# A four-layer graph network on one core: longer lags between producers and consumers, byte flags kept in SBUF, and the last layer's product moved ahead of its scan

## The chip, the cores and the metric

The kernel runs on one core of a Trainium2 chip. The metric is the device time of one execution in microseconds (us). A run of the kernel before takes 7871.08 us, the median of three (7854.48 to 7896.73).

## The reference, cut to what matters

The graph has 100,000 nodes and 50,000 edges sorted by receiver (`dst`), and 128 channels per node, all f32. Four graph layers follow each other, each with a residual and a layer norm over the channels:

```python
edge_index = jnp.stack([src, dst])
x = _layernorm(x + _L0_gnn_ref(x, edge_index, ...))        # attention over 4 heads
x = _layernorm(x + _L1_gnn_ref(x, Wq, Wk, Wv, Wo, edge_index))   # N = 625 nodes in its own formula, all edges
x = _layernorm(x + _L2_gnn_ref(x, edge_index, W0, b0, W1, b1))   # two degree-normalised layers with relu
x = _layernorm(x + _L3_gnn_ref(x, edge_attr_3, edge_weight, src, dst, 100000, ...))   # messages, segment sum, W_out0/W_out1
```

In all of them the messages of the edges with the same receiver are summed (`segment_sum`). In the last one a message has 256 channels (64 scalars and 64 vectors of 3), and the sum is multiplied by the output weights, which leaves 128 channels. A node that receives no edge takes part only through its own row.

## The kernel before

The 50,000 edges are padded to 50,176 = 98 items of 512 edges (4 chunks of 128 edges, one edge per partition). The core works through twelve stages, each with its own buffers and semaphores and a barrier behind it. The change touches the last four, and two small stages ahead of them. In the trace the tiles have these prefixes:

- `ats` is `second_layer`: load the messages `xs`, weight them (GpSimd, `weight`), turn them so that channels lie on partitions (TensorE, `turn`), running sum along the edges (VectorE, `scan`), product with `wvo` (TensorE, `multiply`), add and layer norm (VectorE `add` and `scale`, ScalarE `norm_root` and `apply`, GpSimd `widen`), store.
- `gs0` is `gcn_first`: gather rows by index (GpSimd, four indirect DMAs an item), turn and accumulate with the own rows, scan, product with `w0`, `take`, `activate`, store.
- `gs1` is `gcn_second`: the same with `w1`; a product with only four weight rows (`root` and `blocks`) adds the bias; relu, residual and norm follow.
- `mss` is `final_edges`: gather, scale and turn the sender's row (`scale_x`, `turn_x`, `copy_x`), `project`, build the message of 2 x 128 channels (`messages`), turn both halves (`turn_sums`), two scans, eight products with `wout` (`reduce`), `combine`, norm, and a scatter to the output (GpSimd, four indirect DMAs an item).
- `l0` (`first_layer`), `asc` (`attention_scores`) and `rad` (`radial_basis`) come before these.

The scan multiplies the running sum by a flag that is 0 where a new receiver begins and adds the next message. The flags stand in one line in DRAM, `T["cont"]`, as f32; each of the four stages loads 512 of them per item, copied to all 128 partitions (256 KB), in the same `load` as its other inputs.

Each engine runs a program of its own, written with `pipeline(engine, (part, lag), ...)`: in slot q it does each part, in the order listed, for item q minus its lag. The engines meet only through semaphores (`wait_ge`, and `wait_item(..., 4)` for a buffer that item minus 4 must have left; there are `BUFS = 4` buffers, and two PSUM buffers `tp` and `hp`). An engine's queue is in order, so a waiting part holds up all that stand behind it. In `ats` the lags before are:

```python
            pipeline(sp, (load, 0), (store, 5))
            pipeline(pool, (widen, 3), (weight, 0))
            pipeline(pe, (multiply, 1), (turn, 0))
            pipeline(act, (apply, 4), (lambda t, u: norm_root(norm, act, t, u), 3))
            pipeline(dve, (scan, 0), (add, 1), (scale, 2))
```

`load` there waits for `weighted`, `scanned` and `summed` of the item four back, and then issues all three loads. `apply` writes two tables from `y`: the next layer's input (`t12`, rows of 132 floats, 528 bytes) and the residual (`x2`, rows of 512 bytes), each by four activations. GpSimd's `scatter` in `mss` follows its gathers by `SCATTER_LAG = 4` items.

Of the kernel before, what the change touches and what calls it, by code (L numbers as in the profile page):

```python
# [15 lines left out]
ALU = mybir.AluOpType  # L16
# [25 lines left out]
SCATTER_LAG = 4  # L42
# [143 lines left out]
def edge_line(table, t, u):  # L186

    return table[0:1, bass.ds(t * (4 * BUFS * P) + u * 4 * P, 4 * P)].broadcast_to([P, 4 * P])
# [11 lines left out]
def prepare(nc, A, T, K):  # L200

    with ExitStack() as ctx:
# [15 lines left out]
        same = sb("same", [P, 4, P])  # L218
        final = sb("final", [P, 4, P])
# [42 lines left out]
        def _(sp):  # L262
# [23 lines left out]
            for tile, a, off in [(cur, 1, 0), (nxt, 1, 1), (srow, 0, 0)]:  # L286
# [4 lines left out]
                         same[0:rows].rearrange("p b i -> p (b i)")).then_inc(cont_stored, 16)  # L291
# [3 lines left out]
        def _(act):  # L295
# [10 lines left out]
            act.dma_start(T["cont"][0:1, 0:1], zeros[0:1, 0:1]).then_inc(cont_stored, 16)  # L306
# [33 lines left out]
        def _(dve):  # L340
# [13 lines left out]
            dve.memset(K["row0"][0:1, :], 1.0)  # L354
            dve.memset(K["one"][:], 1.0)
# [21 lines left out]
            dve.tensor_tensor(same[0:rows], cur[0:rows], nxt[0:rows], ALU.is_equal).then_inc(same_ready, 1)  # L377
# [767 lines left out]
def gat_sums(nc, A, T, K):  # L1145
    with ExitStack() as ctx:
# [38 lines left out]
        def _(dve):  # L1185
# [28 lines left out]
            link(dve.tensor_scalar(K["degepsB"][:], K["totB"][:, HEADS, :], 1.0, EPS * D, ALU.add, ALU.mult))  # L1214
# [368 lines left out]
def second_layer(nc, A, T, K):  # L1583
    with ExitStack() as ctx:
# [4 lines left out]
        cont = [sb(f"cont{u}", [P, 4 * P]) for u in range(BUFS)]  # L1589
# [3 lines left out]
        o2 = [sb(f"o2{u}", [P, 4, D]) for u in range(BUFS)]  # L1593
        rsz, nbz = [sb(f"rsz{u}", [P, 4]) for u in range(BUFS)], [sb(f"nbz{u}", [P, 4]) for u in range(BUFS)]
        rsx, nbx = [sb(f"rsx{u}", [P, 4]) for u in range(BUFS)], [sb(f"nbx{u}", [P, 4]) for u in range(BUFS)]
        tp = [ps(f"tp{v}", [P, 4, P]) for v in range(2)]
        hp = [ps(f"hp{v}", [P, 4, D]) for v in range(2)]
        xs_loaded, own_loaded, cont_loaded, weighted = sems("xs_loaded"), sems("own_loaded"), sems("cont_loaded"), sems("weighted")
        turned, scanned, multiplied, summed = sems("turned"), sems("scanned"), sems("multiplied"), sems("summed")
        stored, x_stored, o_set, zero_set = sems("stored"), sems("x_stored"), sem("o_set"), sem("zero_set")  # L1600
# [5 lines left out]
        def _(sp):  # L1606
            def load(t, u):
# [3 lines left out]
                sp.dma_start(xs[u][:], edge_rows(T["xsrc"], t, u)).then_inc(xs_loaded[u], 16)  # L1611
                sp.dma_start(cont[u][:], edge_line(T["cont"], t, u)).then_inc(cont_loaded[u], 16)
                sp.dma_start(own[u][:], edge_rows(T["t12"][0:EP], t, u)[:, :, 0:D]).then_inc(own_loaded[u], 16)

            def store(t, u):
                sp.wait_ge(applied[u], t + 1)
                sp.dma_start(edge_rows(T["t12"][T12_Z:T12_Z + EP], t, u), o[u][:]).then_inc(stored[u], 16)
                sp.dma_start(edge_rows(T["x2"], t, u), o2[u][:]).then_inc(x_stored[u], 16)
            pipeline(sp, (load, 0), (store, 5))
            for u in range(BUFS):  # L1620
                sp.wait_ge(stored[u], 16 * PER_BUF[u])
                sp.wait_ge(x_stored[u], 16 * PER_BUF[u])

        @block.gpsimd
        def _(pool):
# [5 lines left out]
            def widen(t, u):  # L1631
# [3 lines left out]
                pool.tensor_tensor(nbz[u][:], norm["nb"][u][:], four(K["dlastB"], t, u), ALU.mult)  # L1635
                pool.tensor_tensor(rsx[u][:], norm["rs"][u][:], four(K["dsqrtB"], t, u), ALU.mult)
                pool.tensor_tensor(nbx[u][:], norm["nb"][u][:], four(K["dsqrtB"], t, u), ALU.mult).then_inc(widened[u], 1)
            pipeline(pool, (widen, 3), (weight, 0))

        @block.tensor  # L1640
        def _(pe):
# [574 lines left out]
```

## Time and profile before

| | |
|---|---|
| runs | 7854.48, 7871.08, 7896.73 us |
| profiled execution | 7874.37 us, of which the span of the core is 7872.4 us |
| TensorE matmul | 4003.5 us busy (51%) |
| VectorE | 3570.1 us (45%) |
| GpSimd | 3751.2 us (48%) |
| ScalarE | 2687.6 us (34%) |
| `ats`, 4686 to 5374 us | 688 us |
| `gs0`, 5374 to 5973 us | 599 us |
| `gs1`, 5973 to 6590 us | 617 us |
| `mss`, 6590 to 7872 us | 1282 us |

No engine is busy for much over half of the span, so the shares of the whole say little: each stage has its own limit. Dividing a stage by its 98 items gives its pitch, and an engine whose work per item is close to that pitch is what limits it. The clock is TensorE's granted clock as a share of 2.4 GHz; 0.5 is 1.2 GHz.

### The profile page before, as it was taken

How to read it: one execution, taken by the hardware profiler on the slowest of the kernel's cores; microseconds unless marked ns; L12 is line 12 of the kernel's file. 1: busy time of each engine (PE TensorE's matmuls, PEld its weight loads, DVE VectorE, ACT ScalarE, POOL GpSimd, SP SyncE). 2: the span in 40 equal slices, each digit the busy share in tenths (PEclk: the TensorE clock that was granted, in tenths of full speed). 3: DMA queues.
4: the chain of work that ended last, by engine and by line, in shares of the span. 5: the costliest groups of instructions: out<-in, count | busy, mean ns of one | idle time of the engine just before them, and what ended most of it. 6: DMA issues, size and time to landing. Idle time of an engine off the chain costs nothing. (4 is left out here: it accounts for less than half of the span.)

```text
span 7872.4 us, 85274 instructions
## 1 busy us (share of the span) xinstructions
PE 4003.5 (51%) x18822; PEld 3174.7 (40%) x18822; DVE 3570.1 (45%) x12700; ACT 2687.6 (34%) x6766; POOL 3751.2 (48%) x4124
## 2 busy tenths in 40 slices
PE   2444444112961118825468764444556885555555
PEld 1443344101641015514356543333554554555554
DVE  4484444001671005548711135553334665656665
ACT  0014455001861018815433324442222332222222
POOL 3655655775006750003255532225665664666665
PEclk9655555555985559957789975556666666777676
DMA  1236666111851016624455547776777996333333
GB/s 51 64 89 184 185 191 188 36 19 48 262 174 34 21 39 216 216 64 132 110 132 151 158 129 193 190 192 155 178 180 183 220 218 150 98 101 98 101 98 79
DMA packets 1395766, 1048.50 MB, mean 133 GB/s; under 512 B 171017, under 2 KB 1232586, under 8 KB 1395521
## 3 DMA queue, kind: packets, MB, share of 16 engines
q1 hardware_dynamic: 1279294, 866.89, 39.6%
q0 software_dynamic: 112896, 179.36, 10.1%
q10 hardware_dynamic: 3458, 1.02, 0.1%
q14 instruction: 86, 0.70, 0.0%
q8 instruction: 32, 0.52, 0.0%
HBM read 603.60 MB, written 448.78 MB: 134 GB/s over the span
## 5 line engine op out<-in xcount | busy, mean ns | idle before, releaser
L985 POOL DMA_INDIRECT t_alpha<-gsm_raw,gsm_edge_idx x392 | 401.8, 1025 | 591.7 <-DVE gsm_raw L1107 467.2
L1128 PE MATMUL gsm_zr<-kept_ident,gsm_zT 128*128 128x128 f32 x784 | 141.0, 307 | 936.8 <-ACT gsm_zT L1030 749.4
L1952 POOL DMA_INDIRECT out_dram<-mss_o,kept_scat_idx x392 | 390.8, 997 | 364.6 <-ACT mss_o L1297 274.0
L511 POOL DMA_INDIRECT sort_xd<-in_x_dram,kept_dst_idx x392 | 378.6, 966 | 382.9 <-DMA t_xdst<-sort_xd 226.6
L1417 POOL DMA_INDIRECT asc_xs<-t_t,kept_idx_a x392 | 370.8, 946 | 354.2 <-issue 120.3
L1336 POOL TENSOR_TENSOR l_xb<-l_x,kept_bias 128x512 f32<-128x512 f32 x98 | 133.5, 1363 | 842.0 <-DMA l_x<-t_xdst 841.3
L741 PE MATMUL sort_sps<-kept_wa,sort_xdT 128*128 128x4 f32 x784 | 221.6, 353 | 607.0 <-ACT sort_xsT L765 572.8
L1128 PEld LDWEIGHTS gsm_zr<-kept_ident,gsm_zT 128*128 128x128 f32 x784 | 89.8, 150 | 986.9 <-ACT gsm_zT L1030 797.3
L1822 POOL DMA_INDIRECT gs_xs<-t_z,kept_idx_a x392 | 370.7, 946 | 237.0 <-issue 94.0
L1724 POOL DMA_INDIRECT gs_xs<-t_t,kept_idx_b x392 | 370.7, 946 | 214.6 <-issue 105.8
L978 POOL DMA_INDIRECT gsm_raw<-t_al,gsm_from_idx x392 | 395.6, 1009 | 161.5 <-issue 129.1
L1960 POOL DMA_INDIRECT mss_xs<-t_x,kept_idx_a x392 | 396.5, 1011 | 150.7 <-issue 119.2
L741 PEld LDWEIGHTS sort_sps<-kept_wa,sort_xdT 128*128 128x128 f32 x784 | 209.5, 327 | 641.0 <-ACT sort_xsT L765 400.3
L1070 DVE SCALAR_TENSOR_TENSOR gsm_y<-gsm_hp,gsm_x 128x512 f32<-128x512 f32 x196 | 135.5, 692 | 697.4 <-remote 569.3
L513 POOL DMA_INDIRECT sort_xs<-in_x_dram,kept_src_idx x392 | 379.4, 968 | 120.3 <-issue 119.9
L1297 ACT ACTIVATE mss_o<-mss_y,mss_nb,mss_rs 128x128 f32<-128x128 f32 x392 | 161.4, 482 | 756.7 <-DVE mss_nb L1289 451.1
L1030 ACT ACTIVATE gsm_zT<-gsm_zp,kept_b0col 128x512 f32<-128x512 f32 x196 | 134.7, 687 | 754.7 <-remote 477.2
L1511 DVE CUSTOM_DVE_ANT_0 asc_prod<-asc_qp,asc_xs 128x128 f32<-128x128 f32 x392 | 90.6, 287 | 557.3 <-remote 269.7
L1973 PE MATMUL mss_xtp<-kept_ident,mss_xk 128*128 128x128 f32 x392 | 106.1, 423 | 447.9 <-ACT mss_xk L2006 423.0
L1297 ACT ACTIVATE gsm_o<-gsm_y,gsm_nb,gsm_rs 128x128 f32<-128x128 f32 x784 | 323.2, 488 | 15.9 <-issue 15.6
L193 PE MATMUL gs_tp<-kept_ident,gs_xs 128*128 128x128 f32 x784 | 303.9, 394 | 46.3 <-issue 29.4
L1996 PE MATMUL mss_op<-kept_wout,mss_sc 128*128 128x128 f32 x1568 | 311.8, 383 | 4.0 <-DVE mss_sc L2045 4.0
(527 smaller groups left out, 12860.5 us busy)
## 6 DMA issues: line engine op xcount, KB each, us to landing
t_t<-sort_o SPq DMA_DIRECT2D x66, 792.0 KB
t_x<-gsm_o SPq DMA_DIRECT2D x196, 264.0 KB
sort_x<-in_x_dram SPq DMA_DIRECT2D x66, 768.0 KB
gsm_x<-t_t SPq DMA_DIRECT2D x196, 256.0 KB
t_z<-gsm_z SPq DMA_DIRECT2D x196, 256.0 KB
out_dram<-gsm_o SPq DMA_DIRECT2D x196, 256.0 KB
gs_cont<-t_cont SPq DMA_DIRECT2D x196, 256.0 KB
t_t<-l_o SPq DMA_DIRECT2D x98, 264.0 KB
```

The costliest lines, as they stand in the source:

```text
L511: pool.indirect_dma_start(xd[u][:, j, :], None, A["x"], bass.IndirectOffsetOnAxis(K["dst_idx"][:, c:c + 1], 0)).then_inc(gathered[u], 16)
L513: pool.indirect_dma_start(xs[u][:, j, :], None, A["x"], bass.IndirectOffsetOnAxis(K["src_idx"][:, c:c + 1], 0)).then_inc(gathered[u], 16)
L741: pe.matmul(sps[:, j, 0:HEADS], xdT[u % 2][:, j, :], K["wa"][:, HEADS:8], start=True, stop=False)
L978: pool.indirect_dma_start(raw[:, c, 0:HEADS], None, T["al"], bass.IndirectOffsetOnAxis(from_idx[:, c:c + 1], 0)).then_inc(gathered[u], 16)
L985: pool.indirect_dma_start(T["alpha"], bass.IndirectOffsetOnAxis(edge_idx[:, c:c + 1], 0), raw[:, c, :], None).then_inc(scattered[u], 16)
L1297: ac = act.activation(norm["o"][u][:, g, :], norm["y"][u][:, g, :], ACT.Identity, bias=norm["nb"][u][:, g:g + 1], scale=norm["rs"][u][:, g ...
L1417: pool.indirect_dma_start(xs[u][:, j, :], None, T["t12"][0:EP + N], bass.IndirectOffsetOnAxis(K["idx_a"][:, c:c + 1], 0)).then_inc(gathere ...
L1724: pool.indirect_dma_start(xs[u][:, j, :], None, T["t12"], bass.IndirectOffsetOnAxis(K["idx_b"][:, c:c + 1], 0)).then_inc(gathered[u], 16)
L1822: pool.indirect_dma_start(xs[u][:, j, :], None, T["z1"], bass.IndirectOffsetOnAxis(K["idx_a"][:, c:c + 1], 0)).then_inc(gathered[u], 16)
L1952: pool.indirect_dma_start(T["out"], bass.IndirectOffsetOnAxis(K["scat_idx"][:, c:c + 1], 0), o[u][:, j, :], None, bounds_check=N - 1, oob_ ...
L1960: pool.indirect_dma_start(xs[u][:, j, :], None, T["x3"], bass.IndirectOffsetOnAxis(K["idx_a"][:, c:c + 1], 0)).then_inc(gathered[u], 16)
L1996: mm = pe.matmul(op[u % 2][:, j, :], sc[u][:, a, j * P:(j + 1) * P], K["wout"][:, a, :], start=(a == 0), stop=(a == parts - 1))
```

## The change

The lags between the parts grow in all four stages and the parts that shared one `load` are split, each with its own wait. The flags become bytes, are loaded once (in `rad`) to a tile of 50,176 bytes on every partition, and the scans read them there; `m0g` and `emb` are freed after `asc` to make room. `ats` no longer writes `x2`; `gs1` reads its residual from `t12` instead, which holds the same rows scaled by `dlastB`, and makes up for the factor with `dinv2B`, the degree term of the norm, and a new ScalarE part, `lift`. In `mss` the product with `wout` is made on the turned message, ahead of the scan: ScalarE copies the turned halves to SBUF (`copy_msg`), TensorE multiplies (`reduce`, two products with 512 moving columns), VectorE scans one row of 128 channels instead of two, and TensorE turns the result back (`turn_back`).

```diff
-SCATTER_LAG = 4
+SCATTER_LAG = 15
...
+def goes_on(K, t, u):
+    return K["cont"][:, bass.ds(t * (4 * BUFS * P) + u * 4 * P, 4 * P)]
...
# prepare
-            dve.tensor_tensor(same[0:rows], cur[0:rows], nxt[0:rows], ALU.is_equal).then_inc(same_ready, 1)
+            link(dve.tensor_tensor(same[0:rows], cur[0:rows], nxt[0:rows], ALU.is_equal))
+            dve.tensor_copy(same8[0:rows], same[0:rows]).then_inc(same_ready, 1)
...
# gat_sums
-            link(dve.tensor_scalar(K["degepsB"][:], K["totB"][:, HEADS, :], 1.0, EPS * D, ALU.add, ALU.mult))
+            link(dve.tensor_tensor(K["dinv2B"][:], K["dinvB"][:], K["dinvB"][:], ALU.mult))
+            link(dve.tensor_scalar(K["degepsB"][:], K["dinv2B"][:], EPS * D, None, ALU.mult))
...
# radial_basis, on SyncE, behind the loads of r and ahead of those of m0g
+            sp.dma_start(K["cont"][:], T["cont"][0:1, 0:EP].broadcast_to([P, EP])).then_inc(cont_loaded, 16)
...
# second_layer
-                wait_item(sp, weighted, t, u, 4)
-                wait_item(sp, scanned, t, u, 4)
-                wait_item(sp, summed, t, u, 4)
-                sp.dma_start(cont[u][:], edge_line(T["cont"], t, u)).then_inc(cont_loaded[u], 16)
-                sp.dma_start(edge_rows(T["x2"], t, u), o2[u][:]).then_inc(x_stored[u], 16)
-            pipeline(sp, (load, 0), (store, 5))
+            pipeline(sp, (load_xs, 0), (load_own, 3), (store, 10))
-                pool.tensor_tensor(rsx[u][:], norm["rs"][u][:], four(K["dsqrtB"], t, u), ALU.mult)
-                pool.tensor_tensor(nbx[u][:], norm["nb"][u][:], four(K["dsqrtB"], t, u), ALU.mult).then_inc(widened[u], 1)
-            pipeline(pool, (widen, 3), (weight, 0))
+            pipeline(pool, (weight, 0), (widen, 6))
-            pipeline(pe, (multiply, 1), (turn, 0))
+            pipeline(pe, (multiply, 3), (turn, 1))
-                    ac = act.activation(o2[u][:, j, :], y[u][:, j, :], ACT.Identity, bias=nbx[u][:, j:j + 1], scale=rsx[u][:, j:j + 1])
-            pipeline(act, (apply, 4), (lambda t, u: norm_root(norm, act, t, u), 3))
+            pipeline(act, (lambda t, u: norm_root(norm, act, t, u), 5), (apply, 7))
-            pipeline(dve, (scan, 0), (add, 1), (scale, 2))
+            pipeline(dve, (scan, 2), (add, 4), (scale, 5))
...
# gcn_first: no cont load; the parts otherwise as before
-            pipeline(sp, (load, 0), (store, 3))
+            pipeline(sp, (load, 0), (store, 7))
-            pipeline(pe, (multiply, 1), (turn, 0))
+            pipeline(pe, (multiply, 2), (turn, 0))
-            pipeline(act, (activate, 2))
+            pipeline(act, (activate, 4))
-            pipeline(dve, (scan, 0), (take, 1))
+            pipeline(dve, (scan, 1), (take, 3))
...
# gcn_second
-            pipeline(sp, (load, 0), (store, 4))
+            pipeline(sp, (load_own, 0), (load_root, 1), (load_x, 3), (store, 9))
-            pipeline(pe, (multiply, 1), (turn, 0))
+            pipeline(pe, (multiply, 2), (turn, 0))
+            def lift(t, u):
+                act.wait_ge(multiplied[u], t + 1)
+                wait_item(act, summed, t, u, 4)
+                for j in range(4):
+                    ac = act.activation(r[u][:, j, :], hp[u % 2][:, j, :], ACT.Relu, scale=K["dinv2B"][:, bass.ds(4 * BUFS * t + 4 * u + j, 1)])
+                ac.then_inc(lifted[u], 1)
-                dve.scalar_tensor_tensor(out=y[u][:], in0=hp[u % 2][:], scalar=0.0, in1=x2[u][:],
-                                         op0=ALU.max, op1=ALU.add).then_inc(summed[u], 1)
+                dve.tensor_tensor(y[u][:], r[u][:], x2[u][:], ALU.add).then_inc(summed[u], 1)
+            pipeline(act, (norm_root, 5), (lift, 3), (norm_apply, 6))
-            pipeline(dve, (scan, 0), (add, 1), (norm_scale, 2))
+            pipeline(dve, (scan, 1), (add, 4), (norm_scale, 5))
...
# final_edges
-            pipeline(sp, (load, 0), (load_y, 2))
+            pipeline(sp, (load, 0), (load_y, 7))
             def reduce(t, u):
-                pe.wait_ge(scanned[u], t + 1)
-                wait_item(pe, combined, t, u, 2)
-                for j in range(4):
-                    for a in range(parts):
-                        mm = pe.matmul(op[u % 2][:, j, :], sc[u][:, a, j * P:(j + 1) * P], K["wout"][:, a, :], start=(a == 0), stop=(a == parts - 1))
-                mm.then_inc(reduced[u], 1)
+                pe.wait_ge(msg_copied[u], t + 1)
+                wait_item(pe, scanned, t, u, 1)
+                for a in range(parts):
+                    mm = pe.matmul(rp[:], K["wout"][:, a, :], mT[u % 2][:, a, :], start=(a == 0), stop=(a == parts - 1))
+                mm.then_inc(reduced_t[u], 1)
+
+            def turn_back(t, u):
+                pe.wait_ge(scanned[u], t + 1)
+                wait_item(pe, combined, t, u, 2)
+                for j in range(4):
+                    tr = pe.transpose(op[u % 2][:, j, :], sc[u][:, j * P:(j + 1) * P], K["ident"][:])
+                tr.then_inc(reduced[u], 1)
-            pipeline(pe, (reduce, 2), (turn_sums, 1), (turn_x, 0), (project, 0))
+            pipeline(pe, (turn_x, 1), (turn_back, 9), (project, 3), (reduce, 7), (turn_sums, 5))
+            def copy_msg(t, u):
+                act.wait_ge(sums_turned[u], t + 1)
+                wait_item(act, reduced_t, t, u, 2)
+                for a in range(parts):
+                    ac = act.copy(mT[u % 2][:, a, :], tp[:, a].rearrange("p j i -> p (j i)"))
+                ac.then_inc(msg_copied[u], 1)
-            pipeline(act, (norm_apply, 4), (norm_root, 3), (scale_x, 0), (copy_x, 0))
+            pipeline(act, (copy_x, 2), (copy_msg, 6), (norm_root, 11), (scale_x, 0), (norm_apply, 12))
-                for a in range(parts):
-                    sn = dve.tensor_tensor_scan(sc[u][:, a, :], cont[u][:], tp[:, a].rearrange("p j i -> p (j i)"),
-                                                sc[(u - 1) % BUFS][:, a, 4 * P - 1:4 * P], ALU.mult, ALU.add)
+                dve.tensor_tensor_scan(sc[u][:], goes_on(K, t, u), rp[:], sc[(u - 1) % BUFS][:, 4 * P - 1:4 * P],
+                                       ALU.mult, ALU.add).then_inc(scanned[u], 1)
-            pipeline(dve, (scan, 1), (messages, 0), (combine, 2), (norm_scale, 3))
+            pipeline(dve, (scan, 8), (messages, 4), (combine, 10), (norm_scale, 11))
```

(`norm_root`, `norm_scale` and `norm_apply` stand here for the lambdas that call them.)

## Rows read from the trace of the kernel before

**Rows 1.** Windows: stretch, length; PE, PEld, DVE, ACT, POOL busy; clock, DMA share, GB/s.

```profile
4686.00:5374.00 688.00, 312.18 (x1176) 244.72 (x1176) 356.39 (x1279) 331.99 (x883) 161.41 (x490) 0.50 0.73 188
5374.00:5973.00 599.00, 324.20 (x1568) 291.46 (x1568) 225.73 (x491) 125.27 (x392) 370.74 (x392) 0.68 0.70 173
5973.00:6590.00 617.00, 489.36 (x1764) 340.16 (x1764) 377.82 (x1378) 179.90 (x490) 370.74 (x392) 0.63 0.89 210
6590.00:7872.00 1282.00, 708.46 (x3528) 630.72 (x3528) 753.88 (x2157) 353.93 (x980) 787.25 (x784) 0.70 0.37 97
```

**Rows 2.** Timeline of VectorE through one item of `ats`: start, duration, operation, [idle before].

```profile
5340.39 1.28 DVE L1678 TENSOR_TENSOR_SCAN ats_sc<-ats_cont,ats_sc,ats_tp 128x512 f32<-128x512 f32 x1 [3.01 <-PE ats_tp L1646]
...
5344.03 0.16 DVE L1289 SCALAR_TENSOR_TENSOR ats_nb<-ats_mv,ats_rs 128x4 f32<-128x4 f32 x1
5347.13 1.28 DVE L1678 TENSOR_TENSOR_SCAN ats_sc<-ats_cont,ats_sc,ats_tp 128x512 f32<-128x512 f32 x1 [2.93 <-PE ats_tp L1646]
```

**Rows 3.** Waits in `ats`: total us, times, longest.

```profile
POOL ats_rsz L1634 <- DVE ats_nb L1289: 512.3, 98, 7.2
```

**Rows 4.** Timeline of the start of `ats`: GpSimd's product beside a scan.

```profile
4696.03 1.04 POOL L1629 TENSOR_TENSOR ats_xw<-ats_xs,kept_wB 128x512 f32<-128x512 f32 x1 [1.29 <-DMA ats_xs<-t_xsrc]
4696.06 1.28 DVE L1678 TENSOR_TENSOR_SCAN ats_sc<-ats_cont,ats_sc,ats_tp 128x512 f32<-128x512 f32 x1 [3.02 <-PE ats_tp L1646]
```

**Rows 5.** Timeline of `l0`: GpSimd's sum beside a small VectorE operation.

```profile
3873.54 1.27 POOL L1336 TENSOR_TENSOR l_xb<-l_x,kept_bias 128x512 f32<-128x512 f32 x1 [3.09 <-DMA l_x<-t_xdst]
...
3873.69 1.14 DVE L1260 TENSOR_TENSOR l_diff<-l_stats 128x4 f32<-128x4 f32 x1
```

**Rows 6.** DMA in `l0`, 3480 to 3880 us: packets, MB, share of 16 engines.

```profile
q1 hardware_dynamic: 100496, 50.67, 46.8%
```

**Rows 7.** DMA in `asc`, 4000 to 4600 us, and one of three issues.

```profile
q1 hardware_dynamic: 138661, 68.86, 41.0%
...
asc_xd<-t_t SPq DMA_DIRECT2D x87, 256.0 KB
```

**Rows 8.** DMA in `ats`, 4700 to 5340 us.

```profile
q1 hardware_dynamic: 209135, 122.52, 74.7%
```

**Rows 9.** DMA in `gs1`, 6030 to 6550 us.

```profile
q1 hardware_dynamic: 149262, 91.06, 74.7%
q0 software_dynamic: 11052, 22.66, 19.0%
```

**Rows 10.** The gathers of `gs0` and of `gs1`: min/median/max ns, first and last start.

```profile
L1724 POOL DMA_INDIRECT gs_xs<-t_t,kept_idx_b x392: 941/947/987, 5376.3 to 5952.1; - x196
...
L1822 POOL DMA_INDIRECT gs_xs<-t_z,kept_idx_a x392: 939/947/960, 5974.1 to 6559.8; - x196
```

**Rows 11.** `gs1`: 20 us of the windows view, and TensorE groups by line.

```profile
6274.00:6294.00 20.00, 18.11 (x64) 12.40 (x65) 13.38 (x52) 5.50 (x15) 13.03 (x14) 0.53 0.96 217
...
L1861 PE MATMUL gs_hp<-gs_blocks,gs_root 4*128 4x512 f32 x196 | 162.3, 919 | 0.0
```

**Rows 12.** Timeline of GpSimd through one item of `mss`.

```profile
7207.34 1.02 POOL L1952 DMA_INDIRECT out_dram<-mss_o,kept_scat_idx  x1 [2.88 <-ACT mss_o L1297]
...
7212.56 1.30 POOL L1960 DMA_INDIRECT mss_xs<-t_x,kept_idx_a  x1 [0.30 <-issue]
...
7219.97 1.02 POOL L1952 DMA_INDIRECT out_dram<-mss_o,kept_scat_idx  x1 [2.33 <-ACT mss_o L1297]
```

**Rows 13.** Groups of `mss` by line: busy us, mean ns.

```profile
L1996 PE MATMUL mss_op<-kept_wout,mss_sc 128*128 128x128 f32 x1568 | 311.8, 383 | 4.0 <-DVE mss_sc L2045 4.0
...
L2012 ACT COPY mss_xsT<-mss_xtp 128x512 f32<-128x512 f32 x98 | 57.5, 586 | 132.6 <-PE mss_xtp L1973 117.8 <-remote 13.7 <-issue 1.2
```

**Rows 14.** Timeline of `rad`, whose last operation ends the stage.

```profile
3930.48 3.42 DVE L2101 TENSOR_SCALAR rad_inside<-rad_r 64x6272 f32<-64x6272 f32 x1 [22.67 <-DMA rad_r<-t_ew]
...
3949.68 6.68 DVE L2104 TENSOR_TENSOR kept_emb<-rad_r,rad_inside 64x6272 f32<-64x6272 f32 x1 [12.33 <-ACT rad_r L2112]
```

More of the change, by code:

```diff
@@ L290, in _ @@
             sp.dma_start(T["cont"][0:1, 1:EP + 1].rearrange("a (p f) -> (a p) f", f=4 * P),
-                         same[0:rows].rearrange("p b i -> p (b i)")).then_inc(cont_stored, 16)
+                         same8[0:rows].rearrange("p b i -> p (b i)")).then_inc(cont_stored, 16)
             sp.wait_ge(cont_stored, 32)
@@ L1634, in widen @@
                 pool.tensor_tensor(rsz[u][:], norm["rs"][u][:], four(K["dlastB"], t, u), ALU.mult)
[L1635 to L1638 removed]
+                pool.tensor_tensor(nbz[u][:], norm["nb"][u][:], four(K["dlastB"], t, u), ALU.mult).then_inc(widened[u], 1)
+            pipeline(pool, (weight, 0), (widen, 6))
         @block.tensor
@@ L1800, in gcn_second @@
         x2 = [sb(f"x2{u}", [P, 4, D]) for u in range(BUFS)]
-        cont = [sb(f"cont{u}", [P, 4 * P]) for u in range(BUFS)]
+        r = [sb(f"r{u}", [P, 4, D]) for u in range(BUFS)]
         root = [sb(f"root{u}", [4, P]) for u in range(BUFS)]
@@ L1866, in _ @@
             pe.wait_ge(blocks_set, 64)
-            pipeline(pe, (multiply, 1), (turn, 0))
+            pipeline(pe, (multiply, 2), (turn, 0))
         @block.scalar
         def _(act):
+            def lift(t, u):
[4 more added lines that the diff above has]
+                ac.then_inc(lifted[u], 1)
             act.wait_ge(o_set, BUFS)
-            pipeline(act, (lambda t, u: norm_apply(norm, act, t, u, stored), 3), (lambda t, u: norm_root(norm, act, t, u, bias=K["zero"]), 2))
+            pipeline(act, (lambda t, u: norm_root(norm, act, t, u, bias=K["zero"]), 5), (lift, 3), (lambda t, u: norm_apply(norm, act, t, u, stored), 6))
         @block.vector
@@ L1897, in _ @@
             dve.wait_ge(zero_set, 1)
-            pipeline(dve, (scan, 0), (add, 1), (lambda t, u: norm_scale(norm, dve, t, u), 2))
+            pipeline(dve, (scan, 1), (add, 4), (lambda t, u: norm_scale(norm, dve, t, u), 5))
     end_stage(nc, owned)
@@ L1912, in final_edges @@
         xk = [sb(f"xk{u}", [P, 4, D]) for u in range(2)]
-        cont = [sb(f"cont{u}", [P, 4 * P]) for u in range(BUFS)]
         y = [sb(f"y{u}", [P, 4, D]) for u in range(BUFS)]
         o = [sb(f"o{u}", [P, 4, D]) for u in range(BUFS)]
-        sc = [sb(f"sc{u}", [P, parts, 4 * P]) for u in range(BUFS)]
+        sc = [sb(f"sc{u}", [P, 4 * P]) for u in range(BUFS)]
+        mT = [sb(f"mT{v}", [P, parts, 4 * P]) for v in range(2)]
         msg = [sb(f"msg{v}", [P, 4, 2 * D]) for v in range(2)]
@@ L2057, in _ @@
             dve.wait_ge(zero_set, 1)
-            pipeline(dve, (scan, 1), (messages, 0), (combine, 2), (lambda t, u: norm_scale(norm, dve, t, u), 3))
+            pipeline(dve, (scan, 8), (messages, 4), (combine, 10), (lambda t, u: norm_scale(norm, dve, t, u), 11))
     end_stage(nc, owned)
@@ L2088, in _ @@
             sp.wait_ge(w_loaded, 128)
+            sp.wait_ge(cont_loaded, 16)
         @block.vector
@@ L2164, in kept @@
         K[n] = sb(n, [P, 1])
-    for n in ("dstB", "lastB", "ids", "dinvB", "dsqrtB", "dlastB", "degepsB", "wB", "kB"):
+    for n in ("dstB", "lastB", "ids", "dinvB", "dinv2B", "dsqrtB", "dlastB", "degepsB", "wB", "kB"):
         K[n] = sb(n, [P, CHUNKS])
@@ L2181, in build @@
         K = kept(sb)
+        radial = ExitStack()
         for stage in STAGES[:stop]:
             if stage is radial_basis:
-                K["m0g"] = sb("m0g", [P, 8, P])
-                K["emb"] = sb("emb", [P, EIGHTS * P])
+                K["cont"] = sb("cont", [P, EP], mybir.dt.uint8)
+                sb_radial = stage_makers(nc, radial, "kept")[0]
+                K["m0g"] = sb_radial("m0g", [P, 8, P])
+                K["emb"] = sb_radial("emb", [P, EIGHTS * P])
             stage(nc, A, T, K)
+            if stage is attention_scores:
+                radial.close()
 STAGES = [prepare, scores_and_sort, gat_softmax, gat_sums, first_layer, radial_basis, attention_scores, attention_softmax,
```

76 lines of the change are left out of this document (33 added, 43 removed).

## The prediction, made before the changed kernel ran

> **What bounds the kernel now.** I read the windows view by stage first. In none of the four changed stages does an engine fill the time: in `ats` the busiest, VectorE, has 356 of 688 us, in `gs0` GpSimd 371 of 599, in `mss` GpSimd 787 of 1282 [rows 1]. Only `gs1` is near two limits, DMA at 0.89 and TensorE at 489 of 617 us [rows 1]. The reader is to see there that three stages wait on a loop and not on an engine.
>
> Then the waits and the timeline, to find the loop. In `ats` GpSimd's `widen` waits 512 us, 98 times, for VectorE's last operation of a slot [rows 3]; `weight` of the newest item stands behind it, TensorE's `turn` needs `weight`, and VectorE's next scan needs `turn`. So VectorE works from 5340.39 to 5344.19, 3.80 us, and is idle for 2.93 us of a pitch of 6.74 us, the round trip through GpSimd and TensorE [rows 2]. In `mss` the timeline shows the scatter waiting on ScalarE's norm of the item only four back: 2.88 and 2.33 us of a pitch of 12.63 us [rows 12]. In `gs0` the gathers start over 575.8 us, 5.89 us an item [rows 10]: TensorE turns item q, waits for its scan, then multiplies it ahead of turning q+1.
>
> **The change, part by part.** For each stage I take the slowest engine's work per item as the new pitch, after walking the new lags once: every part now waits for something made at least one slot earlier (in `ats`: turn in slot 1, scan 2, product 3, sum 4, scale 5, `widen` 6, `apply` 7, store 10), or in the same slot for a part that stands first on the other engine. Buffer waits of four items reach back three slots or more, but for the product's two PSUM buffers, which are emptied a slot before. I find no loop that takes longer than one slot of the slowest engine.
>
> `ats`: VectorE's slot of 3.80 us remains [rows 2]. ScalarE loses four of eight activations, GpSimd two of five operations, the queue of SyncE two of five transfers; none is on the path, so they are priced at nothing by themselves. TensorE has 312/98 = 3.2 us an item at a clock of 0.50 [rows 1], below 3.8, so it stays covered. New is that GpSimd's product (1.04 us) runs beside VectorE's work. At the stage's start the two lay beside each other, and the scan kept 1.28 us [rows 4]; in `l0` a small VectorE operation beside GpSimd's sum took 1.14 us [rows 5], where one of its size takes 0.16 [rows 2]. The product follows `widen`, so it starts some 0.4 us into the scan and ends 0.2 us behind it: I take 0.2 us an item, with ends 0 and 1.04. DMA: in `l0` a packet costs 0.468 x 400 x 16 / 100,496 = 29.8 ns of an engine [rows 6]; a transfer of 512 rows (528 packets with the 16 of its semaphore, worked out from the 16 increments in the code) costs all 16 engines 0.98 us. Three remain: 2.95 us, below the pitch. New pitch 4.0 us (3.8 to 4.85). Gain 98 x (6.74 - 4.0) = 268 us, less 5 for a longer run-out: **263** (180 to 283).
>
> `gs0`: GpSimd bounds it. A gather is 0.947 us [rows 10] and the gap behind it 0.30 us [rows 12], four make 5.0 us. TensorE has 3.3 us, VectorE 2.3, ScalarE 1.3 an item [rows 1], DMA 0.70 x 5.89 = 4.1 us less one flag load. The own rows' load no longer stands behind a store that waits for ScalarE. Gain 98 x 0.89 = 87, less 2: **85** (60 to 88).
>
> `gs1`: the pitch is 585.7/391 x 4 = 5.99 us [rows 10]. Of DMA's (0.747 + 0.190) x 520 us [rows 9], 5.6 us an item, the flag load is one part. Its price: what q1 has over row transfers at 0.98 us is 1.5 us here (0.747 x 5.99 less three) and 1.1 us in `ats` (0.747 x 6.74 less four [rows 8]). So 4.1 to 4.5 us remain: no more the bound. TensorE has 489/98 = 5.0 us an item at 0.63 [rows 1], GpSimd 5.0. ScalarE gets `lift`, four activations, near 1.3 us by `gs0` (125/98) on top of 1.8, and VectorE reads its sum's operand from SBUF instead of PSUM, its 3.9 us unchanged; both covered. Two engines at 5.0 don't fit perfectly: 5.15. Gain 98 x 0.84 = 82, less 2: **80** (30 to 95).
>
> Here the clock matters. In 20 us with TensorE busy for 18.11, the granted clock was 0.53, so mostly the lower level of 1.2 GHz; the product with four weight rows is 1.66 us of each item's 5.0 [rows 11]. I keep the clock where it is. The Trainium skill (TensorE: Matmul & The Clock Gate, What's actually happening) says that activity releases the throttle; by it a stage with fewer pauses runs at 2.4 GHz. Rows 11 speak against it for this mix. By the rule the pitch would be GpSimd's 5.0, 15 us better (rival e).
>
> `mss`: GpSimd again. The scatters of one item take 5.22 us (7207.34 to 7212.56, one gap included) and the gathers that follow 5.4 (7212.56 to 7219.97 less the 2.33 idle, whose first 0.30 is the ordinary gap) [rows 12]: 10.6 us. Moved and added work: VectorE loses one scan of 1.28 us of its 7.7 an item. ScalarE gets two copies of 0.59 us [rows 13] on 3.6. TensorE trades eight products (311.8/98 = 3.2 us [rows 13]) for two with the same columns and gets four turns, between 0 and one `turn` of `ats` with its tail, 1.1 us: 7.2 + 1.1 = 8.3. All are below 10.6, and the scatter has three slots of slack. Gain 98 x 2.03 = 199; the 31 us that the first scatter waits now for the first results are filled with gathers of 15 items. Less some 10 because these gathers outrun the 6 to 8 us slots of the other engines: **215** (120 to 225).
>
> Outside: `prepare` gets one conversion and `gat_sums` one small product, 1 us. In `rad` 50,176 bytes for each of 128 partitions, 6.4 MB, follow the loads of `r`, which land at 3930 us, 26 us before the stage's last operation ends at 3956.4 [rows 14]. At the flag loads' own rate (0.262 MB in 1.1 to 1.5 us) they need 27 to 37 us, so the cover is short by 1 to 11 us: **-10** (0 to -45; at the rate of small broadcast packets it would be twice as long).
>
> Sum: 263 + 85 + 80 + 215 - 11 = 632. The profiled execution took 7874 us (2 us outside its span, 3 over the median of the runs), so 7874 - 632 = **7242 us**, and the same against the median within 3.
>
> **Rivals.**
> (a) A part of the stages keeps a second limit. GpSimd's product stalls VectorE by all of its 1.04 us in `ats` (4.85: 83 us lost) and DMA keeps `gs1` at 5.6 (44 us lost): 7242 + 127 = 7369. For it: rows 5 and the DMA share of 0.96 in `gs1`. Against: rows 4.
> (b) Reads from rows of 528 bytes are dearer. `gs1` takes its residual from such rows now. No row shows such a price; at half as much again as 0.98 us, as a bound of mine, DMA has 4.6 to 5.0 us an item, and at a share of 0.94 the pitch is up to 5.3 to 5.5: 15 to 35 us lost, 7270. A third of the transfers in `asc` read such rows, and a packet there costs 0.410 x 600 x 16 / 138,661 = 28.4 ns, less than in `l0` [rows 6, 7], so I see no surcharge. The Trainium skill (DMA: Bandwidth & Descriptors, How a descriptor splits into AXI transactions) says that a descriptor off a 256-byte boundary fetches unused bytes; by it 512 bytes become up to 24 beats from 16.
> (c) `mss` becomes bound by TensorE. If the clock falls to 0.5 from 0.70, its 8.3 us become up to 11.6: 98 us lost, 7340. Against: its pauses shorten, not lengthen.
> (d) Slower than before: byte flags slow the scan. No row has a scan of bytes. At X us a scan, `ats` has a slot of 2.7 + X, `gs1` 2.6 + X, `gs0` 1.1 + X, `mss` 6.4 - 1.3 + X. At 3 us 220 us are lost; at about 4.8, 3.8 times the 1.28 of now, all 632 are.
> (e) TensorE is granted 2.4 GHz for most of `gs1`, since it pauses less: 7227. For it: the clock of 0.68 and 0.70 in stages with short pauses; against: rows 11.
>
> **How the numbers follow.** Forecast 0.56, (a) 0.15, (b) 0.08, (c) 0.12, (d) 0.03 (of it 0.02 beyond the deciding point), (e) 0.04, better than the forecast by 40 us or more 0.02. The predicted time is the forecast's, 7242. The range reaches down to the gains' upper ends in part (7242 - 20 - 3 - 15 - 10 = 7194, and some room: 7175) and up to where (a) and (c) lie, 7390; it leaves out both together. A change of under 0.5%, 39 us, can't be told from none: that needs 590 us of the gains to be lost. Faster 0.96, same 0.01, slower 0.03.
>
> **What would show it.** In the profile after: `ats` at about 420 us with VectorE almost without idle time; `gs0` and `gs1` at 515 and 537, their gathers 5.0 and 5.15 us an item apart; `mss` at 1067, its scatters without the waits on ScalarE; q1 without flag loads, and the scan's mean at 1.28 us. What makes it wrong: idle time in front of the first part of a slot on any engine (a loop that I missed), VectorE operations of 1 us beside GpSimd's product, a scan over 1.28 us, or a `rad` stage longer by more than 45 us.

## The result, and the profile after it

The changed kernel took **7597.67 us** (median of 4 runs, 7573.39 to 7606.5) beside 7880.42 for the kernel before: a ratio of **0.9639** (95% interval 0.9603 to 0.9675), 3.6% faster. The forecast was 7242 us with a range of 7175 to 7390. The gain has the forecast sign and less than half of its size: 301 us between the two profiled spans (7872.4 and 7571.4), where the sum had 632.

The windows view of the changed kernel, cut at its stages `rad`, `asc`, `ats`, `gs0`, `gs1`, `mss` (columns as in [rows 1]):

```profile
3893.00:3957.00 64.00, 0.00 (x0) 0.00 (x0) 20.02 (x7) 12.70 (x5) 0.13 (x1) 0.50 0.61 130
3957.00:4647.00 690.00, 540.96 (x3131) 414.87 (x3132) 117.95 (x980) 236.74 (x392) 369.84 (x392) 0.91 0.57 150
4687.00:5088.00 401.00, 205.88 (x1176) 177.49 (x1176) 357.54 (x1279) 181.20 (x491) 132.56 (x294) 0.77 0.74 194
5088.00:5680.00 592.00, 297.81 (x1568) 281.41 (x1568) 222.29 (x491) 125.02 (x392) 369.78 (x392) 0.69 0.51 132
5680.00:6294.00 614.00, 433.13 (x1764) 301.47 (x1764) 378.34 (x1378) 281.98 (x882) 396.87 (x392) 0.70 0.65 169
6294.00:7571.00 1277.00, 589.27 (x2744) 427.41 (x2744) 631.69 (x2059) 441.41 (x1176) 768.92 (x784) 0.71 0.29 77
```

`ats` fell from 688 to 401 us, as forecast and a little more: VectorE now works 358 of 401 us. The other three stages kept their times: 599 to 592, 617 to 614, 1281 to 1277 (`mss` of before is cut here at 6591 us, 1 us later than in [rows 1]). Yet the change was made in them: DMA's share fell from 0.70, 0.89 and 0.37 to 0.51, 0.65 and 0.29, and VectorE lost its second scan in `mss`. No engine is near its limit in any of the three. They have in common that GpSimd issues indirect transfers in them.

What the idle time is can be read where a stage stands still. The timeline of `gs0` (start, duration, operation, idle before it and who ended it):

```profile
5112.47 0.27 PE L194 MATMUL gs_tp<-kept_ident,gs_own 128*128 128x128 f32 x1
...
5121.11 0.42 PE L194 MATMUL gs_tp<-kept_ident,gs_own 128*128 128x128 f32 x1
...
5124.08 0.94 POOL L1718 DMA_INDIRECT gs_xs<-t_t,kept_idx_b  x1 [0.30 <-issue]
5129.51 1.28 DVE L1770 TENSOR_TENSOR_SCAN gs_sc<-kept_cont,gs_sc,gs_tp 128x512 f32<-128x512 uint8 x1 [11.87 <-DMA t_t<-sort_o]
5129.74 0.94 POOL L1718 DMA_INDIRECT gs_xs<-t_t,kept_idx_b  x1 [4.72 <-DMA t_t<-sort_o]
```

The reader is to see two things. The scan and the gather at 5129.5 both wait for `turned` of one item, and by the semaphore numbers in the trace that item's transposes are those that ended at 5112.74: the increment is recorded at 5129.48, 17 us later. In the meantime TensorE turned the next item (to 5121.53), and from 5125.02, the end of the last gather's issue, to 5129.51 no engine works. And the view names as releaser a transfer of the sort stage, thousands of us earlier. That is no cause; it is the sign that no nearby instruction's end fits the release. TensorE has 196 instructions in `gs0` that send an increment. For 175 of them the trace holds an increment ahead of the next one of the same semaphore; laid beside the recorded ends, 133 of these (76%) arrive more than 1 us late, and half of the 175 more than 4.5 us. In `ats` it is none of 196. And it is TensorE's signals alone: in `gs0` none of the 150 recorded increments of VectorE and none of the 83 of ScalarE comes more than 0.02 us after the end of its instruction. The Trainium skill (Perfetto Trace Analysis, Tensor Engine Instruction) says that a matmul's recorded end is computed and that the semaphore follows when PSUM has acknowledged the bytes; by that a record's end promises nothing of the signal, and this trace agrees in the gather stages (17 us above). So it can't tell a signal that travels late from a write to PSUM that is confirmed late; "late" below means late after the recorded end.

### The profile page after: what moved, and what is told of

It is laid out like the page before. It is cut to its first block and busy times, and to the rows that moved or that the text cites. A ratio compares the mean times of both kernels' runs of the same rounds, so it can differ in the third digit from the quotient of the medians.

```text
span 7571.4 us, 82465 instructions
## 1 busy us (share of the span) xinstructions
PE 3689.6 (49%) x18038; PEld 2854.1 (38%) x18038; DVE 3444.5 (45%) x12605; ACT 2725.2 (36%) x6962; POOL 3722.9 (49%) x3928
## 5 line engine op out<-in xcount | busy, mean ns | idle before, releaser
L1815 POOL DMA_INDIRECT gs_xs<-t_z,kept_idx_a x392 | 396.9, 1012 | 206.3 <-issue 107.8
L1959 POOL DMA_INDIRECT mss_xs<-t_x,kept_idx_a x392 | 377.7, 964 | 166.5 <-issue 118.4
L1302 ACT ACTIVATE sort_o<-sort_x,sort_nb,sort_rs 128x128 f32<-128x128 f32 x792 | 312.2, 487 | 0.0
L1749 PE MATMUL gs_hp<-kept_w,gs_sc 128*128 128x128 f32 x784 | 171.9, 391 | 273.7 <-DVE gs_y L1777 209.9
L1292 DVE RECIPROCAL gsm_rs<-gsm_sd 128x4 f32<-128x4 f32 x196 | 34.8, 178 | 578.7 <-ACT gsm_sd L1044 314.2
L193 PE MATMUL gs_tp<-kept_ident,gs_xs 128*128 128x128 f32 x784 | 268.9, 359 | 54.4 <-DMA gs_xs<-t_t,kept_idx_b 27.7
```

Of the source, the lines that this page charges most:

```text
L193: pe.matmul(out, lhsT=a, rhs=ident[:], start=True, stop=False, is_transpose=True)
L1302: ac = act.activation(norm["o"][u][:, g, :], norm["y"][u][:, g, :], ACT.Identity, bias=norm["nb"][u][:, g:g + 1], scale=norm["rs"][u][:, g ...
L1815: pool.indirect_dma_start(xs[u][:, j, :], None, T["z1"], bass.IndirectOffsetOnAxis(K["idx_a"][:, c:c + 1], 0)).then_inc(gathered[u], 16)
L1959: pool.indirect_dma_start(xs[u][:, j, :], None, T["x3"], bass.IndirectOffsetOnAxis(K["idx_a"][:, c:c + 1], 0)).then_inc(gathered[u], 16)
```

## The experiments

In some sets of runs the kernel before took 7830 to 7884 us, as in the first measurement, in the others 6391 to 6410. I call the first condition *late* and the second *prompt*. No run shows what decides between them: the same chip number occurred in both. Runs are compared only within a condition.

**1. The three stages with their old distances and order**, `ats` and the resident flags kept.

```
gs0:  pipeline(pe, (multiply, 2), (turn, 0))      -> (multiply, 1), (turn, 0)
      pipeline(dve, (scan, 1), (take, 3))         -> (scan, 0), (take, 1)
gs1:  (scan, 1), (add, 4), (norm_scale, 5)        -> (scan, 0), (add, 2), (norm_scale, 3)
mss:  two scans, then reduce, as before; SCATTER_LAG 15 -> 4
```

The distances of the other engines in these stages go back too. `lift` stays in `gs1`, so VectorE's last two parts there stand one slot later than in the kernel before.

> The changed kernel with the distances of gs0, gs1 and mss put back to those of before, the second scan of mss and its old reduction back, byte flags from the resident tile kept; only ats keeps its new distances. In the changed profile gs0 took 592 us (before 599), gs1 614 (617), mss 1277 (1282). Theory A, the three gather stages gained nothing from the change because something that both orders share sets their pitch: 7590 to 7630 us, the three stages within 10 us each of the changed kernel's. The prediction's sum (distances worth 85, 80 and 215 us in them, lost somewhere else in the changed kernel): 7700 us or more.

These runs were prompt, so no expectation in us can be read from it directly: 6071.41 us, ratio 0.9501 (0.9486 to 0.9517). Run again under the late condition:

> The changed kernel with gs0, gs1 and mss at the distances and the order of before. Late increments: the three stages keep the changed kernel's times within 15 us each, since the lateness and not the distances sets them, so 7590 to 7640 us. In time: 6071 us as before, 250 to 300 above the changed kernel, all of it in mss.

7554.02 us, ratio 0.9647 (0.9629 to 0.9664), beside 7554.17 for the changed kernel measured with it; `gs0`, `gs1` and `mss` take 589, 610 and 1281 us with the old distances and 583, 607 and 1291 with the new. Under the late condition the new distances in `gs0`, `gs1` and `mss` are worth nothing that can be measured. Under the prompt one they are worth 245 us (6071 less the changed kernel's 5826, experiment 4), and the windows put them all in `mss`: 1275 us with the old order, 1021 with the new, while `gs0` and `gs1` have 502 and 527 us with the old distances and 504 and 529 with the new.

**2. Plain rows in place of the indirect gathers.** The indices are left out in `gs0` and `gs1`; GpSimd issues the same bytes by plain transfers, or SyncE does.

```
-  pool.indirect_dma_start(xs[u][:, j, :], None, T["t12"], IndirectOffsetOnAxis(idx_b[:, c:c + 1], 0))
+  pool.dma_start(xs[u][:, j, :], T["t12"][c * P:c * P + P, :])
```

> Leaves out the indices in gs0 and gs1: GpSimd issues four plain transfers of 128 rows for an item in place of the four indirect gathers, same bytes, same buffers, same waits. Theory A1, increments of TensorE's semaphores are held back while GpSimd works through indirect transfers: the held increments go and gs0 falls from 592 to 430 us or less and gs1 to 540 or less, if GpSimd's plain issue is under 1 us. Rival A2, any transfer that GpSimd issues does it: gs0 stays within 560 to 620 with increments still seconds late. Rival A3, the buffer loop gather, landing, turn, gather over four buffers sets the pitch: gs0 stays 570 to 600 with the landing unchanged, and increments in time.

> Leaves out the indices in gs0 and gs1 and GpSimd's part altogether: the SyncE queue issues the four transfers of 128 rows. GpSimd is idle. Theories A1 and A2: TensorE's increments arrive with the end of the instruction, as in ats; gs0 98 times 4.0 to 4.4 us, 390 to 430 us; gs1 500 to 540. Rival A3 (buffer loop): gs0 still above 550. If SyncE's six transfers for an item bound it (0.37 to 0.50 us each), gs0 is still below 430.

(In the first of these "seconds late" should read microseconds.) Both fell on the prompt condition, where nothing was late to begin with, so they tell no cause: `gs0` 243 and 354 us (less than the 390 that was expected of the second), `gs1` 438 and 430. The form was run again under the late condition, from GpSimd in `gs0` and from SyncE in `gs1`:

> Leaves out the indices in gs0 and gs1: in gs0 GpSimd issues four plain transfers for an item, in gs1 SyncE does and GpSimd is idle. Late increments: if indirect generation is what holds them, they are in time in both, gs0 about 230 to 250 us and gs1 about 400; if any transfer of GpSimd's does, they stay late in gs0 (450 us or more) and are in time in gs1. In time anyway: gs0 227 and gs1 about 410 us between first and last transfer, as in the two runs that had these forms.

7067 us. Its windows of `gs0` and `gs1`:

```profile
5070.00:5320.00 250.00, 199.23 (x1568) 178.32 (x1568) 222.67 (x497) 125.13 (x392) 206.86 (x392) 0.96 1.05 313
5320.00:5760.00 440.00, 385.52 (x1764) 264.28 (x1764) 373.98 (x1372) 279.06 (x879) 0.00 (x0) 0.78 0.92 235
```

`gs0` falls from 583 us to 250 with GpSimd still issuing 392 transfers, the first to the last start in 226.9 us, as under the prompt condition (226.6). None of TensorE's 196 increments in it is over 1 us late, and none in `gs1`; in `mss` of the same run, whose transfers are still indirect, 229 of the 438 recorded ones are. So neither GpSimd's issuing of transfers nor the buffers' loop does it; indirect transfers do. The plain rows are also consecutive ones, so whether it is the indirect form itself or the scattered rows that it reads was not separated.

**3. More buffers.** `gs0` with eight SBUF buffers and four PSUM tiles of each kind, `gs1` with four PSUM tiles.

```
-  wait_item(pool, turned, t, u, 4)        +  wait_item(pool, turned, t, u, 8)
-  wait_item(pe, scanned, t, u, 2)         +  wait_item(pe, scanned, t, u, 4)
-  tp[u % 2], hp[u % 2]                    +  tp[u % 4], hp[u % 4]
```

> Nothing left out. gs0 has eight buffers of everything in SBUF and four PSUM tiles of each kind; gs1 keeps four buffers and gets four PSUM tiles of each kind. Rival A3 (buffer loop): gs0 becomes GpSimd's bound, 98 times 5.0 plus 20, 510 us, gs1 (PSUM only) stays near 614. Theory A1 or A2 (increments held until GpSimd pauses): GpSimd pauses more rarely, and each pause still costs the 2 to 4 us in which nothing runs, so gs0 530 to 580; gs1 590 to 614. Total 7500 to 7580.

> The kernel with eight SBUF buffers and four PSUM tiles in gs0, and four PSUM tiles in gs1. Late increments: if the fixed number of buffers turns the lateness into stalls, gs0 falls from 572 to 500 to 540 and gs1, whose buffers for gathered rows stay four, by at most 20; if increments come through only in GpSimd's pauses, the pauses stay and gs0 is 550 or more. In time: gs0 489 and gs1 505 as before, no more than 10 us from the changed kernel in all, since GpSimd's issue is the bound with four buffers already.

Prompt: 5820.15 us, ratio 0.9107 (0.9092 to 0.9122), `gs0` 503, `gs1` 532. Late: 7553.0 us, 0.9638 (0.9622 to 0.9654), `gs0` 583 and `gs1` 610 where the changed kernel measured with it has 583 and 607. Twice the buffers buy nothing in either condition. It was the one candidate for a kernel better than both, and it is none.

**4. The two kernels in both conditions.**

> The kernel before, unchanged, for a trace of the conditions under which the four experiments ran: there it took 6391 us, not 7880, and in them TensorE's semaphore increments were not late. If the lateness is a property of the conditions and not of a kernel: 6391 us within 0.5 percent, with the three gather stages at gs0 500 to 530, gs1 510 to 560, mss 1230 to 1280, and under 5 percent of TensorE's increments more than 1 us late. If the conditions of the first measurement return: 7870 us and more than half of them late.

> The changed kernel, unchanged. With increments in time: gs0 490 and gs1 505 us as in the run with more buffers, mss 925 to 940, ats 400, in all 5800 to 5840 us, a ratio of 0.908 to 0.914 to the kernel before, of which ats and the flags are 320 us and mss 300. The prediction's sum scaled to these conditions has the same order (632 us of gain in place of 282). If the late increments return: 7597 us and a ratio of 0.964.

> The changed kernel, unchanged, beside the three experiments of this call. Two conditions have been seen: one in which TensorE's semaphore increments arrive late in the stages with indirect transfers (kernel before 7880 us), one in which they arrive in time (before 6391). Late: 7600 us, ratio 0.964 to 0.967. In time: gs0 490, gs1 505, mss 925, total 5800 to 5840 us, ratio 0.908 to 0.914.

The first two fell on the late condition: 7874.86 us, and 7610.68 with a ratio of 0.9658 (0.9645 to 0.9672). So did the third, 7554.17 us, 0.9646 (0.9628 to 0.9663). The first measurement is repeated. The prompt condition was met later:

> The changed kernel. In time: 5800 to 5840 us, ratio 0.908 to 0.914, gs0 489, gs1 502 to 505, mss 925 us from first to last gather. Late: 7555 to 7610, ratio 0.964 to 0.967, a repeat.

> The kernel before, unchanged, for its stages. In time (6391 us): the changed kernel took 489 us in gs0, 505 in gs1, 1007 from the first gather to the last scatter in mss, in all 5826, so 570 us of difference are spread over ats, gs0, gs1 and mss: ats 280, gs0 and gs1 10 to 30 each by GpSimd's bound, mss 250 to 280. Late: 7830 to 7880 and gs0 576, gs1 587, as twice before.

Changed 5825.81 us, ratio **0.9111** (0.9096 to 0.9126); before 6411.08 in one run. The stages `ats`, `gs0`, `gs1`, `mss` of the kernel before, prompt:

```profile
3375.00:4062.00 687.00, 309.85 (x1176) 242.66 (x1176) 355.80 (x1274) 331.96 (x883) 161.40 (x490) 0.50 0.74 188
4062.00:4565.00 503.00, 290.55 (x1568) 251.38 (x1568) 225.76 (x491) 125.23 (x392) 370.80 (x392) 0.71 0.80 206
4565.00:5134.00 569.00, 479.65 (x1764) 322.14 (x1764) 377.69 (x1378) 179.99 (x490) 370.80 (x392) 0.63 0.92 228
5134.00:6409.00 1275.00, 703.39 (x3528) 625.07 (x3528) 753.33 (x2157) 355.14 (x980) 786.45 (x784) 0.70 0.37 97
```

and of the changed kernel, prompt:

```profile
3368.00:3769.00 401.00, 204.69 (x1176) 175.62 (x1176) 356.87 (x1275) 181.20 (x491) 132.64 (x294) 0.77 0.74 194
3769.00:4273.00 504.00, 278.54 (x1568) 256.50 (x1568) 225.70 (x491) 125.00 (x392) 370.01 (x392) 0.77 0.61 155
4273.00:4802.00 529.00, 414.20 (x1764) 282.30 (x1764) 376.94 (x1378) 280.61 (x882) 383.29 (x392) 0.72 0.77 196
4802.00:5823.00 1021.00, 578.75 (x2744) 434.45 (x2744) 628.87 (x2059) 438.93 (x1176) 772.13 (x784) 0.82 0.36 96
```

`ats` is the same to 1 us in either condition. `gs0` gains nothing here too, for another reason: the kernel before already ran it at GpSimd's 5.0 us an item. The waits of `gs0` in the changed kernel, first prompt:

```profile
POOL gs_xs L1718 <- issue: 119.1, 391, 0.3
```

```profile
DVE gs_sc L1770 <- PE gs_tp L194: 272.6, 97, 8.5
```

then late:

```profile
POOL gs_xs L1718 <- issue: 103.0, 338, 0.3
POOL gs_xs L1718 <- DMA t_t<-sort_o: 79.6, 44, 4.7
POOL gs_xs L1718 <- DMA asm_rows<-t_w: 19.4, 9, 2.8
```

```profile
DVE gs_sc L1770 <- DMA t_t<-sort_o: 287.8, 47, 11.9
DVE gs_sc L1770 <- DMA asm_rows<-t_w: 58.4, 9, 7.3
DVE gs_sc L1770 <- PE gs_tp L194: 16.4, 4, 8.5
```

Prompt, GpSimd waits for nothing but its own 0.30 us between two issues, and the scan's idle time is put down to the transposes that it waits for. Late, both wait for signals whose sender has, by its recorded end, long been done.

**5. Is it a price of the indirect transfer, or of everything beside it?** A stage with the 392 gathers alone was added, and in `gs1` the gathers wait for nobody and nobody reads them; another kernel leaves out the indices of every second group of 128 rows.

```
new stage, GpSimd only:  wait_item(pool, gathered, t, u, 4, 64); four indirect gathers of an item
gs1:  -  wait_item(pool, turned, t, u, 4)      +  wait_item(pool, gathered, t, u, 4, 64)
gs1:  -  pe.wait_ge(gathered[u], 64 * t + 64)
gs1:  -  accumulate_turned(.., xs, own, ..)    +  accumulate_turned(.., own, own, ..)
half: j = 0, 2 indirect; j = 1, 3 plain, from GpSimd in gs0, from SyncE in gs1
```

> Adds a stage between gs0 and gs1 with the 392 gathers of gs0 alone: GpSimd waits only for the landing four items back, and no other engine works. In gs1 the gathers wait only for their own landing too and nobody reads them: the sums add each own row twice, so the gathered rows are left out of the result; all other work is there. Late increments, theory A1 (work of indirect transfers delays every semaphore increment): in gs1 TensorE's increments are still late although no wait links it to the gathers, and gs1 takes over 450 us; the lone stage takes 489 to 525 us. Rival A4 (each indirect transfer costs 1.43 us on this chip whatever else runs): the lone stage takes 560 us, and TensorE's increments in gs1 are in time. Rival A3 (buffer loop): the lone stage 489, gs1's other work about 400 as with plain rows. In time: lone stage 489, gs1 489 to 500.

> Leaves out the indices of every second group of 128 rows: in gs0 GpSimd issues two indirect and two plain transfers for an item, in gs1 two indirect ones and SyncE two plain ones. With all four plain gs0 took 227 us between its first and last transfer, with all four indirect 562 to 572 (late) or 489 (in time). If each indirect transfer carries its own 1.43 us: 98 times (2 times 1.43 plus 2 times 0.58), 394 us in gs0, and gs1 about 410, bound by the other work. If the lateness needs indirect transfers back to back without a pause, it goes in gs1, where GpSimd works 2.5 of 4.1 us, and TensorE's increments are in time there; if it does not, gs1 takes 480 or more.

> The kernel with a stage of 392 gathers alone added, and in gs1 gathers that nobody reads. With increments in time it measured 489 us alone, 515 in gs1. With late increments, theory A1: alone between 500 and 530, in gs1 over 545 with most of TensorE's increments over 1 us late though no wait links them to the gathers. Rival A4 (own price of an indirect transfer): alone 560 or more, TensorE in time in gs1. Rival A3: alone 489, TensorE in time.

All met the prompt condition, as did three repeats (one of the half-and-half kernel, two more of the other): 489 us for the gathers alone, 515 to 516 in `gs1`, 364 and 401 us with half of them plain. They answer nothing about the late condition; they only confirm GpSimd's 1.25 us an indirect transfer. An answer was in the trace of the kernel before. `gat_softmax` (node work: load, turn, multiply, norm, store) runs beside 392 gathers that no wait ties to it; GpSimd waits only for its own landings four items back. The kernel before, late, during those gathers and after them:

```profile
1390.00:1914.00 524.00, 78.69 (x230) 48.47 (x228) 28.11 (x140) 38.79 (x90) 394.86 (x392) 0.54 0.12 22
1914.00:2381.00 467.00, 339.75 (x1792) 224.37 (x1792) 313.98 (x1357) 320.52 (x799) 0.06 (x1) 0.89 0.64 199
```

and prompt, during the same gathers:

```profile
1146.00:1636.00 490.00, 367.11 (x1970) 243.47 (x1970) 270.08 (x1369) 347.58 (x876) 370.67 (x392) 0.91 0.73 212
```

Late, TensorE gets 79 us of work done in 524 us beside the gathers, and 340 us in 467 as soon as they end; prompt it does 367 us beside them. This is not a price of the gather alone, nor a loop through it. The gather has a small price of its own: the 392 starts spread over 523.8 us late and 489.3 prompt, 1.34 and 1.25 us each.

Which signals are slow can be read in the late trace. Three lines of the same loop, two of TensorE and one of ScalarE:

```profile
1554.76 2.07 PE L1122 MATMUL gsm_zp<-gsm_xT,kept_w 128*128 128x512 f32 x2 [6.74 <-issue]
...
1599.10 0.69 ACT L1030 ACTIVATE gsm_zT<-gsm_zp,kept_b0col 128x512 f32<-128x512 f32 x1 [33.19 <-remote]
...
1599.84 1.12 PE L1128 MATMUL gsm_zr<-kept_ident,gsm_zT 128*128 128x128 f32 x4 [42.15 <-ACT gsm_zT L1030]
```

TensorE's product ends at 1556.84, and its increment is recorded at 1599.07, 42 us later; ScalarE starts at once. ScalarE ends at 1599.78, its increment is recorded at 1599.79, and TensorE starts 0.05 us behind that. The view puts TensorE's 42 us down to ScalarE, which had itself been held by TensorE's signal. In the 524 us 28 of TensorE's 31 recorded increments are over 1 us late, half of them over 42 us, and none of the 22 recorded of VectorE or the 22 of ScalarE. So in this loop the other engines are held by the late signals of TensorE, not by those of each other.

The whole kernel bears it out. Late and prompt, the kernel before takes 1284 and 1040 us in `scores_and_sort`, 1967 and 1084 in `gat_softmax`, 690 and 498 in `asc`, 1212 and 1068 in `gs0` and `gs1` together, all with indirect transfers. Its stages without any agree within 4 us: 128 and 127 in `gat_sums`, 407 and 411 in `l0`, 57 and 57 in `rad`, 685 and 685 in `ats`. The exception is `mss`, with 1272 and 1266 us in spite of its indirect transfers; its old order holds it there in either condition (experiment 1).

## Why the prediction was wrong, and where it was right

| stage | forecast gain | late (the result) | prompt | forecast time | time late, prompt |
|---|---|---|---|---|---|
| `ats` | 263 | 287 | 286 | 425 | 401, 401 |
| `gs0` | 85 | 7 | -1 | 514 | 592, 504 |
| `gs1` | 80 | 3 | 40 | 537 | 614, 529 |
| `mss` | 215 | 4 | 254 | 1067 | 1277, 1021 |
| elsewhere | -11 | 0 | 7 | | |

Each gain is the difference of two windows; they add up to 301 and 586 us, the differences of the spans.

**The step that failed** is "`gs0`: GpSimd bounds it ... four make 5.0 us", and with it the same step of `gs1` and `mss`. The 0.89 us of idle time an item in `gs0` was put down to TensorE's order (turn, wait for the scan, multiply). The kernel before, prompt, has the same order and runs the stage in 503 us, so the order costs nothing there. The idle time was TensorE's late signals, which the distances between parts did not remove: experiments 1 and 3 move `gs0` by 6 us at most. In place of the 1.25 us that the step took for an indirect transfer, start to start, the changed kernel had 1.46 us in `gs0` ((5661.2 - 5090.3)/391) and 1277/784 = 1.63 in `mss`. With the signals in time the step's 5.0 us an item hold (504 us in `gs0`), but there the kernel before had them already, so the gain of 85 would not have come either.

**`ats`** was right in mechanism and 24 us small. The scans are 3.91 us apart on average and not 4.0 (9 us), so the product beside VectorE costs 0.1 us where 0.2 was taken, of its range of 0 to 1.04. Before, they were 6.83 us apart on average ((5353.9 - 4691.8)/97) where one item's 6.74 was taken (9 us more), and the longer run-out of 5 us can't be seen.

**`mss`** has two limits that happened to be equal. The old order holds it at 1275 us prompt and 1281 late; the change removes that limit, as forecast (254 us prompt for the 215 of the sum), and late the signals hold it at 1277. One measured number, two causes: without the prompt runs it would have looked as if the new order did nothing. The prompt 1021 us lie near the forecast 1067: its mechanism holds there, but only with signals in time.

**`gs1`**: late it gained 3, prompt 40, from 569 to 529 us. The old distances give 527 there (experiment 1), so the 40 come from what that experiment kept, the flag loads gone and the product released by ScalarE; which of them isn't separated.

**`rad`**: the flags' load cost nothing; the stage ends at 3957 us as before, where -10 was taken from a range of 0 to -45.

**The rivals.** (a) did not come: `ats` ended below the forecast, and DMA's share in `gs1` fell to 0.65. (b) is out with the same 0.65. (c) is out: TensorE is busy for 589 of 1277 us. (d) is out: the scan of byte flags takes 1.28 us, as before. (e) is out for the result: the clock in `gs1` rose from 0.63 to 0.70 and the time stayed. The time that came belonged to none of them; the list had no case in which the stages keep their idle time.

**Two sums** of the prediction are off, by too little to matter: the terms given for `mss` (199 + 31 - 10) make 220 and not 215, and a scan of 3 us in rival (d) would cost some 211 us (167 in `ats`, 44 in `gs1`) and not 220.

**What the trace of before could have shown.** Two views spoke and were not read. The waits of VectorE in `gs0` of that trace begin:

```profile
DVE gs_sc L1778 <- remote: 164.2, 34, 13.3
DVE gs_sc L1778 <- PE gs_tp L194: 116.9, 36, 12.4
```

though the program has no remote partner, and that scan waits for TensorE, the flag load and its own chain. And the pair of windows of `gat_softmax` above is from that trace: a loop that the change doesn't touch, at a fifth of its speed beside gathers.

What stays open: why TensorE's signals are late beside indirect transfers in some sets of runs and not in others. No experiment with gathers alone met the late condition. The late traces hold fewer semaphore records than the prompt ones (48,528 and 112,219 for the changed kernel); whether the tracing has a part in the lateness, no run here shows.

## What to carry to other kernels

Before you price an idle gap as a loop of the program, find the signal that ends it and compare it with the end of its sender: where the view names "remote" or a transfer from another stage, or where signals sent many us apart arrive within 0.3 us (as at 5129.4 above), the gap may not be yours to remove by distance. A wait that is put down to one engine can be another's: ask what held that engine. Look in the unchanged stages for the same work with and without the suspected neighbour; one pair of windows costs nothing. And when a change that should act in several stages acts in one, run it where the suspected limit is absent before you call its mechanism wrong: here the same diff is worth 3.6% or 8.9%.

## What the runs showed of the hardware that was not expected

TensorE's semaphore increments can arrive long after the recorded end of the instruction that sends them. Under the late condition half of the recorded ones in `gs0` came over 4.5 us late, and half of those beside the gathers of `gat_softmax` over 42 us; in `ats`, which has no indirect transfer, and in `gs0` with plain ones from GpSimd, none was over 1 us. VectorE's and ScalarE's were in time in `gs0` and in `gat_softmax`; in `gs1` 12 of VectorE's 357 recorded ones were 1 to 3.1 us late, and in `mss` a few more. The same kernel takes 7880 or 6400 us with it or without it; `ats` takes 688 and 687. An indirect transfer of 128 rows costs GpSimd 1.25 us start to start, prompt, a plain one of the same bytes 0.58 (226.9/391), in both conditions for the plain one.
